# A two-layer transformer step on one core: where the fp8 stage's input is normalised, and how its maximum over partitions is taken

## The reference

```python
x = x + L0_attn(layernorm(x), ...)      # gated-slot attention, 16 heads
x = x + L0_ffn(layernorm(x), weight, bias)   # fp8 quantised product
x = x + L1_attn(layernorm(x), ...)      # sliding window of 64
x = x + L1_ffn(layernorm(x), ...)       # routed and shared experts

def L0_ffn(x, weight, bias):
    amax_x = max(abs(x))                 # over the whole tensor
    amax_w = max(abs(weight))
    x_scale = amax_x / (448 * 0.8)
    w_scale = max(amax_x, amax_w) / (448 * 0.8)
    x_dq = fp8(x / x_scale) * x_scale
    w_dq = fp8(weight / w_scale) * w_scale
    return x_dq @ w_dq.T + bias
```

## Time and profile before

| | |
|---|---|
| median of 3 runs | 2098.75 us (2097.74 to 2103.28) |
| the profiled execution | 2093.93 us, of it span 2092.1 us |
| PE busy | 1773.3 us (85%) |
| DVE busy | 1321.9 us (63%) |
| ACT, POOL busy | 801.2 us, 762.7 us |
| `abc_stage`, last group | about 708 to 922.7 us of the span |
| `fp8_stage` | 923.9 to about 976.8 us |

### The profile page before, as it was taken

The page is one execution under the profiler, slowest core; times in us unless marked ns, Lnnn a source line. Parts: engine busy times, 40 slices in busy tenths (PEclk is TensorE's granted clock), DMA queues, the critical chain, the costliest instruction groups (busy, mean ns, idle before and its releaser), DMA issues. The chain is left out here.

```text
span 2092.1 us, 39447 instructions
## 1 busy us (share of the span) xinstructions
PE 1773.3 (85%) x14355; PEld 1494.5 (71%) x14355; DVE 1321.9 (63%) x2657; ACT 801.2 (38%) x1951; POOL 762.7 (36%) x1004
## 2 busy tenths in 40 slices
PE   5999999999999999944899999999985537488870
PEld 3888888888888888832688888888873426377760
DVE  5777787778777787768566666666655416233335
ACT  3444444444444444413355555555554002122220
POOL 3333433343334433343424234233212441255551
PEclk9999999999999999975899999999997659688885
DMA  2100010004900000001100001000005111645435
GB/s 90 46 0 0 1 46 0 0 0 147 235 0 0 2 0 0 0 8 65 41 2 22 21 2 42 2 2 1 1 1 199 64 71 40 175 132 145 149 108 219
DMA packets 72796, 108.87 MB, mean 52 GB/s; under 512 B 24988, under 2 KB 53852, under 8 KB 72028
## 3 DMA queue, kind: packets, MB, share of 16 engines
q1 hardware_dynamic: 62300, 77.51, 12.8%
q0 software_dynamic: 9216, 25.44, 3.4%
q10 hardware_dynamic: 1152, 4.19, 0.5%
HBM read 62.30 MB, written 45.09 MB: 51 GB/s over the span
## 5 line engine op out<-in xcount | busy, mean ns | idle before, releaser
L795 POOL TENSOR_TENSOR a_ms<-a_ms,a_esq 128x4 f32<-128x4 f32 x64 | 14.2, 222 | 447.5 <-DVE a_ms L710 447.5
L1867 POOL DMA_INDIRECT ys<-m_yb,m_dest x128 | 122.7, 958 | 141.2 <-ACT m_yb L1966 105.9
L1250 ACT ACTIVATE b_prob<-b_sc,b_nmax 128x128 f32<-128x128 f32 x256 | 99.7, 391 | 138.7 <-DVE b_nmax L1317 138.7
L1312 DVE SCALAR_TENSOR_TENSOR b_sc<-b_ps_s,window_mask 128x512 f32<-128x512 f32 x64 | 44.3, 692 | 135.6 <-PE b_ps_s L1154 135.6
L1130 PE MATMUL b_ps_u<-xh,b_w_hi 128*128 128x512 f32 x256 | 114.9, 449 | 3.9 <-DVE b_rope L1306 1.9
L596 DVE RECIPROCAL a_rz<-a_ps_sz 128x256 f32<-128x256 f32 x64 | 112.5, 1757 | 3.2 <-PE a_ps_sz L344 3.2
L1921 PE MATMUL m_ps_y<-m_wd,m_hT 64*128 x256 | 77.6, 453 | 37.5 <-ACT m_hT L1959 33.8
L684 DVE TENSOR_TENSOR a_mix_m<-a_ps_av,square_consts 128x512 f32<-128x512 f32 x64 | 44.3, 692 | 98.5 <-PE a_ps_av L430 98.5
L555 ACT ACTIVATE a_sq<-a_ps_og 128x512 f32<-128x512 f32 x64 | 38.2, 597 | 176.8 <-PE a_ps_og L450 161.4
L1385 POOL TENSOR_TENSOR b_Q<-b_rope 128x512 f32<-128x512 f32 x32 | 41.4, 1294 | 168.1 <-DVE b_rope L1306 168.1
L1130 PE MATMUL b_ps_u<-xl,b_w_hi 128*128 128x512 f32 x256 | 102.5, 401 | 0.0
(11 more groups left out here) (335 smaller groups left out, 6082.1 us busy)
## 6 DMA issues: line engine op xcount, KB each, us to landing
xs<-a_zeros SPq DMA_DIRECT2D x32, 528.0 KB, 14.9
m_xb<-xs SPq DMA_DIRECT2D x32, 528.0 KB
wgu_all<-wgu SPq DMA_DIRECT2D x4, 2048.0 KB, 14.2
b_w_raw<-Wb SPq DMA_DIRECT2D x12, 512.0 KB, 5.3
m_wd<-wd SPq DMA_DIRECT2D x2, 2048.0 KB, 17.9
f_got<-ys SPq DMA_DIRECT2D x8, 512.0 KB, 15.7
f_got<-ys ACTq DMA_DIRECT2D x8, 512.0 KB, 14.9
X<-x SPq DMA_DIRECT2D x2, 1024.0 KB, 7.4
```

Of the source, the lines that this page charges most:

```text
L1250: last = nc.scalar.activation(prob[:, n % 2, h, :], sc[:, h % 2, h // 2, :], ACT.Exp, bias=nmax[:, at:at + 1], accum_out=den[:, n % 2, 0, ...
L1867: pool.indirect_dma_start(ys, bass.IndirectOffsetOnAxis(ap=dest[:, i % HOMES, j:j + 1], axis=0), yb[:, i % RING, j // 2, j % 2, :], None). ...
```

## The change

The normalisation moves out of `fp8_stage` into the last group of `abc_stage`. After `measure_tile`, DVE's `y_add` also aggregates that one tile. One step later POOL computes the tile's reciprocal deviation (`rstd_out`: an add and a power over one column), and DVE normalises the tile and takes its maximum (`norm_out`), between `o_low` and the wait for L430. The last two tiles follow behind the last `y_add`. For this the loops of DVE and POOL over steps 2 to 13 become straight code in the last group. The weight and the bias are loaded by SP in `abc_stage`, behind the clearing of `xs`. In `fp8_stage` the maximum over partitions is taken by two turns on TensorE with a row maximum on DVE between them; the bias adds on POOL no longer wait for anything, and still stand ahead of its first subtraction. The tensors for all this live across the two stages.

```diff
@@ abc_stage, SP
             sp.wait_ge(xs_zero, 16 * (NBLK // 4 + 1))
+            sp.dma_start(f_wt[:], A["f_w"].rearrange("(k p) d -> p k d", p=P)).then_inc(f_in, 16)
+            sp.dma_start(f_bias[:], A["f_bias"].unsqueeze(0).broadcast_to([P, D])).then_inc(f_in, 16)
+            sp.wait_ge(f_in, 32)
@@ abc_stage, DVE
                 if final:
                     dve.wait_ge(c["y_add"], done(G))
-                    measure_tile(nc, X, stats, tile)
+                    measure_tile(nc, X, stats, tile).then_inc(c["out_stat"], 1)
+                    dve.wait_ge(c["out_stat"], done(G - LAST))
+                    nc.vector.bn_aggr(out_meanvar[:, ds(tile, 1), :].rearrange("p a b -> p (a b)"),
+                                      stats[:, ds(tile, 1), :]).then_inc(c["out_aggr"], 1)
+
+            def norm_out(G, tile):
+
+                dve.wait_ge(c["out_pow"], done(G - LAST))
+                nc.vector.tensor_scalar(out_n[:, ds(tile, 1), :], X[:, ds(tile, 1), :],
+                                        out_meanvar[:, ds(tile, 1), 0:1].rearrange("p a b -> p (a b)"),
+                                        out_rstd[:, 1, ds(tile, 1)], ALU.subtract, ALU.mult)\
+                    .then_inc(c["out_norm"], 1)
+                dve.wait_ge(c["out_norm"], done(G - LAST))
+                nc.vector.tensor_reduce(out_amax[:, ds(tile, 1)], out_n[:, ds(tile, 1), :], AX, ALU.max,
+                                        apply_absolute_value=True)
...
                 if prev:
                     o_low(H - 1, n)
+                if final and tile_two is not None:
+                    norm_out(H - 2, tile_two)
...
-                with dve.Fori(1, CH - 1) as t:
-                    step(H0 + t * 2, 0, t + CH - 1, final=final)
-                    step(H0 + t * 2 + 1, 1, t, final=final)
+                if final:
+                    for t in range(1, CH - 1):
+                        step(H0 + t * 2, 0, t + CH - 1, final=True, tile_two=t - 1)
+                        step(H0 + t * 2 + 1, 1, t, final=True, tile_two=t + CH - 1)
+                else:
...
             y_add(NG * STEPS - 1, 2 * CH - 1, True)
+            norm_out(NG * STEPS - 2, CH - 1)
+            norm_out(NG * STEPS - 1, 2 * CH - 1)
@@ abc_stage, POOL
+            def rstd_out(G, tile):
+
+                pool.wait_ge(c["out_aggr"], done(G - LAST))
+                hold(pool, held)
+                nc.gpsimd.tensor_scalar(out_rstd[:, 0, ds(tile, 1)],
+                                        out_meanvar[:, ds(tile, 1), 1:2].rearrange("p a b -> p (a b)"), EPS, None,
+                                        ALU.add).then_inc(c["out_eps"], 1)
+                pool.wait_ge(c["out_eps"], done(G - LAST))
+                nc.gpsimd.tensor_tensor(out_rstd[:, 1, ds(tile, 1)], out_rstd[:, 0, ds(tile, 1)], minus_half[:, 0:1],
+                                        ALU.pow).then_inc(c["out_pow"], 1)
...
                 if tile_after_next is not None:
                     chunk(H + 2, b, tile_after_next)
+                if tile_two is not None:
+                    rstd_out(H - 2, tile_two)
                 pool.wait_ge(c["esum_hi"], done(H))
@@ fp8_stage, POOL
-            nc.gpsimd.memset(minus_half[:], -0.5).then_inc(const, 1)
             nc.gpsimd.tensor_copy(ident_b[:], ident).then_inc(const, 1)
-            pool.wait_ge(const, 2)
-            rstd_of(nc, pool, meanvar, rstd, minus_half, aggr, rs, eps_added, held)
-
-            pool.wait_ge(bias_in, 16)
             with pool.Fori(0, NT) as t:
                 xt = X[:, ds(t, 1), :].rearrange("p a d -> p (a d)")
-                pool.wait_ge(normed, t + 1)
                 nc.gpsimd.tensor_tensor(xt, xt, bias[:], ALU.add).then_inc(biased, 1)
-            pool.wait_ge(maxed, 1)
-            nc.gpsimd.partition_all_reduce(amax_all[:], amax[:], P, bass.bass_isa.ReduceOp.max).then_inc(reduced, 1)
@@ fp8_stage, DVE
-            aggregate(nc, stats, meanvar, aggr)
-
-            dve.wait_ge(loaded, 16)
...
-            dve.wait_ge(normed, NT)
-            linked(nc.vector.tensor_reduce(amaxes[:, 0:B], xn[:].rearrange("p (b j) d -> p b (j d)", b=B), AX, ALU.max,
+            linked(nc.vector.tensor_reduce(amaxes[:, NT:NT + 1], wt[:].rearrange("p k d -> p (k d)"), AX, ALU.max,
                                            apply_absolute_value=True))
-            nc.vector.tensor_reduce(amax[:, 0:1], amaxes[:, 0:B], AX, ALU.max)
+            nc.vector.tensor_reduce(amax[:, 0:1], amaxes[:, 0:NT], AX, ALU.max)
             nc.vector.tensor_reduce(amax[:, 1:2], amaxes[:], AX, ALU.max).then_inc(maxed, 1)
-            dve.wait_ge(reduced, 1)
-            linked(nc.vector.tensor_scalar(scale[:], amax_all[:], 1.0 / QMAX, None, ALU.mult))
+            dve.wait_ge(p_max, 1)
+            linked(nc.vector.tensor_reduce(peak[:], psM[:], AX, ALU.max))
+            nc.vector.tensor_copy(peak_all[:], peak[:].broadcast_to([2, P])).then_inc(peaked, 1)
+            dve.wait_ge(p_all, 1)
+            linked(nc.vector.tensor_scalar(scale[:], psA[:, 0:2], 1.0 / QMAX, None, ALU.mult))
@@ fp8_stage, PE
-            pe.wait_ge(const, 2)
+            pe.wait_ge(maxed, 1)
+            nc.tensor.transpose(psM[:], amax[:], ident).then_inc(p_max, 1)
+            pe.wait_ge(peaked, 1)
+            nc.tensor.transpose(psA[:, 0:2], peak_all[:], ident[0:2, 0:2]).then_inc(p_all, 1)
+            pe.wait_ge(const, 1)
             pe.wait_ge(w_quant, 1)
```

89 lines of the change are left out of this document (47 added, 42 removed).

## The result

| | before | changed |
|---|---|---|
| median, runs in turn on one chip | 2101.02 us (2097.74 to 2106.58, 4 runs) | 2078.48 us (2075.68 to 2080.24, 4 runs) |
| ratio, 95% interval | | 0.9889 [0.9862, 0.9916] |
| profiled execution, its span | 2093.93, 2092.1 us | 2080.24, 2078.4 us |

The forecast was 2085.8 us with a range from 2080.5 to 2091.5. The two profiled executions differ by 13.7 us where I had forecast 12.9, the medians by 22.5.

The account below looks back on a forecast made before the run. The prediction took a 25.10 us DVE and POOL chain without PE as the bound. Terms -14.9, +2.15 and -0.15 gave -12.9 us, so 2085.8 us from the 2098.75 us median, range 2080.5 to 2091.5.

Parts of the forecast that it names:

- taking the difference over to the median: Whole kernel: the -12.9 us for the profiled execution was applied to the 2098.75 us median, giving 2085.8 us.
- -15.05: fp8 stage: the first POOL subtraction moves from 30.03 to 15.1 us after stage start, -14.9, with -0.15 behind it.
- +2.15: Attention stage's tail: last aggregation, POOL's add and power, normalisation and maximum add 2.15 us (bounds 1.8 and 2.7).
- the scales: fp8 stage: scales ready 3.4 us after its first DVE instruction (bounds 2.6 and 4.5), where before 23.87.
- the contention of the bias adds: fp8 stage: DVE instructions beside POOL's 16 adds delay them by 3.7 us, so adds end at 15.1, not 11.4.
- The eleven instructions: fp8 stage: eight DVE instructions to the first finished group and three of the second, together 7.9 us, fall beside the adds.
- Full alternation: Rival, fp8 stage: DVE instructions delay adds by their whole duration, first subtraction at 19.3, 2090.1 us; chance 0.12.
- what L894 had waited for: fp8 stage before: POOL's first subtraction, 30.03 us behind the stage's start, was taken to end the DVE and POOL chain.
- No contention: Rival, fp8 stage: adds run at 0.68 us throughout, first subtraction at 11.4, 2082.1 us; chance 0.10.
- Growing steps: Rival, attention stage: 0.1 to 0.4 us more in each of 14 steps, 2087.2 to 2091.4 us; chance 0.13.
- a wait for POOL's power in `norm_out`: Slower rival, attention steps: DVE waits for the power; at 1.4 us a step, 2105.5 us; chance 0.04.
- DVE would wait for PE's turns as long as for the reduction: Rival, fp8 stage: the 4.06 us wait returns for PE, time stays near 2086; no separate chance given.

Follow-up runs that it names:

- the first job: Kernel before, changed kernel and two variants of the partition maximum, in turn on one chip; the unchanged changed kernel measured 2081.43 us, ratio 0.9897.
- the last two jobs: Fourth and fifth sets of runs, with the changed kernel rerun unchanged against the kernel before: 2087.67 us, ratio 0.9948, and 2088.33 us, ratio 0.9950.
- no_bias: Changed kernel without the bias additions, the bias left out of the result: 2069.38 us, ratio 0.9861 to the kernel before.
- pe_turns: Kernel before with only the maximum over partitions taken by TensorE turns: 2092.49 us, ratio 0.9956; repeated later at 0.9984.
- par_end: Changed kernel plus a partition reduction and a small addition on GpSimd in the last stage: 2086.28 us, ratio 0.9946 to the kernel before.
- par_hidden: Changed kernel plus a partition reduction on scratch columns in the very first stage: 2094.42 us, ratio 0.9960 to the kernel before.
- par_idle: Changed kernel plus a partition reduction and a small addition on GpSimd at the window stage's end: 2082.97 us, ratio 0.9924 to the kernel before.

## Why the prediction was right and where it was wrong

**The step that failed: taking the difference over to the median.** The sum of the prediction is one of two stages of one execution, -12.9 us. I took it over to the median as it was, so all other stages stood in it at nothing, for which I gave no reason, and gave the range only the bounds of my terms and "a microsecond or so" for the spread. The measured medians differ by 22.5 us. The two stages account for 10.9 in that pair of traces and for 12.7 in the mean of all. In place of the nothing the runs showed that the same kernel's median moves: 2078.48, 2081.43, 2087.67 and 2088.33 us in four comparisons, its ratio from 0.9889 to 0.9950, while the interval of each is 0.0033 or less to either side. What moves with it is the time at the lower clock level, 361.3 and 361.2 us in the first two comparisons and 370.6 and 371.3 in the last two. In the first job that is 18 us less than the shorter fp8 stage explains, in the last two jobs nothing. Why it falls so stays open. The mean of the four ratios, 0.9921, is 2082.2 us on the base of 2098.75, inside the range; a job like the last two, scaled to that base, would have fallen inside it as well, so which side of the range's edge the first comparison fell on was in part chance.

**What the change itself is worth: 11.2 us, and the agreement of 12.7 with 12.9 is luck.** The fp8 stage is 53.8 to 54.6 us with the old code (4 traces, mean 54.0) and 40.5 to 40.7 with the new (8 traces), -13.4, where the prediction has -15.05 (-14.9 and -0.15). The attention stage is 892.1 us in the mean of 5 traces with the old loop and 892.8 in that of 10 with the new, +0.7 for my +2.15. The sum is -12.7, but the two misses, 1.65 and 1.45, cancel, and the second is none of the change's: cut finer, the stretch from the start of the last L81 to the clearing of the semaphores grew from 0.85 to 3.06 us, to within 0.01 in every trace, +2.2 as forecast; the last group's steps, second to last reciprocal, took 188.3 us in both; and of the 1.5 us, 0.2 lie behind the last reciprocal and 1.3 in the stretch up to the group's second, whose work did not change. It took 675.2 to 677.0 us in the 5 traces and 673.2 to 676.8 in the 10, with 6.8 to 13.7 us of it at the lower level. So -13.4 + 2.2 = -11.2 us is what the change's own rows show, near the 10.4 and 11.8 of the last two jobs.

**Right: the mechanism in its main steps.** The stretch was a chain of DVE and POOL. L929 is released by POOL's own adds; the steps kept their length; the block ended 2.2 us later behind its last statistics (925.90 - 922.05 = 3.85 us to the next stage's first instruction, before 1.62), for which I had 2.15; the scales came 3.33 us into the stage, for which I had 3.4; one column's power took 0.58, estimated at 0.57; the idle time before `a_mix_m` became 0.77 for 0.65; the DMA wait went. no_bias shows DVE alone bringing the first group at 8.5 us, for which I had 9.0.

**Wrong in size: the contention of the bias adds.** I had the 16 adds at 10.9 + 3.7 = 14.6 us and so L929 at 15.1. They took 16.14, it started at 16.62, 1.5 us later, which is nearly all of the fp8 stage's miss. The rule of my estimate, that a DVE instruction holds back the next add by its own duration less 0.36, was read from instructions of 256 columns. The eleven instructions that I had counted are those that fell beside the adds, but those of 0.43, 0.69 and 1.23 us held them back by 0.18 to 0.19, 0.45 and 0.98, their duration less 0.25: 7.9 - 11 x 0.25 = 5.15, and 16.14 - 10.9 = 5.24 was measured. Full alternation would have been 7.9. The other way round DVE was held up as well: L958 and L961 on 1024 columns took 1.10 us, where the same two took 0.69 in no_bias, and L966 took 0.91 for 0.49.

**Missed, with little effect: what L894 had waited for.** I read it as hanging on DVE. It hung on POOL's way back from the reduction's code, 6.79 us, as pe_turns showed. It went by luck: DVE was only 0.57 us ahead.

**The rivals.** No contention (2082.1 us) would have been nearest by the median alone, and is refuted by the trace: 16.14 us of adds. A range's edge that fits is no proof of its mechanism. Full alternation (L929 at 19.3) is refuted by L929 at 16.62. Growing steps are refuted by the steps' length, and a wait for POOL's power in `norm_out` by L629, which stood idle for POOL once, 0.37 us at the last tile, and in no step. That DVE would wait for PE's turns as long as for the reduction did not come: 0.47 and 0.36 us.

## What to carry to other kernels

Work that sits between two blocks because it needs the last tile can often go into the steps before, one tile late, if the engines have waits there; ask then what was hidden beside it, since that (here 16 bias additions) is late next, and can mostly move into the same waits. Idle time before an instruction is not exactly the room in front of it: here 1.06 us in place of 0.77 cost nothing, and what ends the room may be its reader or a later instruction of its own engine. A change of under 1% needs a second job: an interval from runs in turn on one chip tells the spread within the job and not that between jobs. The mean clock of each execution helps to tell the two apart. Rows of the touched stretches are steadier (the fp8 stage agreed within 0.2 us in eight traces, the block's end within 0.01 in ten), but a whole stage with much unchanged work in it is not: the attention stage took from 890.5 to 895.2 us in the changed kernel and its variants with the same code for it.

## What the runs showed of the hardware

- GpSimd's reduction over partitions takes 0.37 us (0.43 in par_end), but stands behind 5.5 to 5.8 us of idle time where the DMA engines were idle, and behind 8.4 in par_hidden and par_end, where they were busy for 0.71 and 0.95 of the stretch.
- The first ordinary instruction behind it comes 6.8 to 7.2 us later in the quiet traces, 7.4 us after the change of configuration in par_hidden, and 11.0 in par_end. That change ran ahead of the instruction's own wait (L894, before), but behind another instruction of the queue that waited (L70, par_hidden). One small ordinary instruction directly behind the reduction, as in par_idle, put both idle times where the engine had nothing to do.
- An add of 256 columns on GpSimd, 0.68 us apart alone, was spaced 0.87, 1.13 and 1.66 us beside DVE instructions that take 0.43, 0.69 and 1.23 us alone: some 0.44 us more than DVE's instruction, and not the full sum of 1.1, 1.4 and 1.9.
- DVE's instruction on one column (L952) took 0.55 us beside a bias addition and 0.16 without it (no_bias's timeline).
- The same code in the experts' stage took from 279.8 to 300.0 us, with a granted clock of 0.80 and 0.75.
